# The first capped experts' front, moved beside the first scan stage chunk by chunk

## The chip, the cores and the metric

The kernel runs on one core of one Trainium2 chip. The metric is the device time of one execution in microseconds: 5519.37 us, the median of three runs (5518.34 to 5522.48). The profile is of one further execution.

## The reference, cut to what matters

Eight layers work on 4 x 1024 tokens of 256 features; each layer's result is added to its input x after a layer norm of x. The first layer is a selective scan (Mamba block), the second a mixture of eight experts with a capacity. Only these two are touched by the change:

```
x = x + mamba_block(layernorm(x), ...)      # scan over the tokens, 512 channels x 16 states
x = x + L0_ffn(layernorm(x), W_router, b_router, experts_inter, experts_out)
def L0_ffn(x):
    logits = x_flat @ W_router.T + b_router ; weights = softmax(logits)
    top_vals, top_idx = top_k(weights, 2)   ; mask = (topk_flat > 0)
    # of each expert the first `capacity` = 640 tokens, in the order of the tokens
    inputs = x_flat[used_tokens] * mask
    out = relu(inputs @ experts_inter[e]) @ experts_out[e]
    combined = zeros.at[used_tokens].add(out * weight)
```

The same experts come a second time behind the third layer (RWKV). A token's row in its expert's block depends on how many earlier tokens chose that expert, so the routing of a part of the tokens needs the counts of the parts before it.

## The kernel before, in words

The 4096 tokens stand as 32 tiles of 128 in the SBUF tile K.X. A chunk is four tiles, so there are eight chunks, 0 to 7. Each layer is a stage with a function of its own that writes one program for each engine: V is DVE, S is ACT, G is POOL, T is PE and Q is the SP queue. An engine carries its instructions out in the order written, and waits on semaphores. At the end of a stage SP waits for all semaphores of the stage and then lets the engines go on (meet_all, barrier).

The scan stage (mamba_stage, with the class Scan): a chunk has 32 units, one for each pair of channel halves and state. In a unit POOL makes the product of dt*u and B for both halves (L435, 128x1024), ACT the two decays (L402) into PSUM, DVE the two scans (L370), then DVE weighs one half with C (L377) and POOL the other (L444); in every fourth unit DVE weighs both. PE sums the weighed halves into PSUM (L477). POOL makes its products three units ahead (AHEAD = 3), the h and B/C tiles are rings of six. The SP queue issues a 512 KB broadcast of B and C for each unit, and in the first units one of 20 transfers of zeros each fourth unit.

All other work of the scan stage is placed beside the units by ticks, two for a unit (0 to 63 in a chunk). Scan.program takes the generators early, front, late and back of the chunks; each yields the tick at which it wants to go on, and `beside(tick)` runs what is due. beside is called twice in a unit on each engine. What has not come to its turn at tick 63 is issued by `beside(whole)` at the chunk's end. back(c), which is the output product of chunk c and its addition to x, is put beside the units of chunk c + 1. The work of one chunk's front (norm, input product, convolution, silu, dt) shares the two PSUM banks called front.

The experts' front is the class CappedFront. For a chunk it has these numbered steps: 0 statistics of the rows on DVE (L221, L225); 1 their factors on POOL (L233 to L244); 2 the normed rows on ACT (L1209); 3 transposes on PE (L1249) and copies on ACT (L1216); 4 the router's product on PE (L1257) and the addition of the bias on DVE (L1146). For a part of several chunks follow: 5 and 6 the softmax and the choice of two experts on DVE (L1157 to L1173, with an exponential on ACT, L1223), 6 the counting product on PE (L1267), 7 the rows' places on DVE (L1180 to L1196), and then on POOL two indirect DMAs for each tile that scatter its rows to DRAM (L1237). The helper `then` makes each DVE instruction of the routing wait for the one before it. Before the change the first experts' front stands in moe0_stage: two parts of four chunks, all behind the scan stage's barrier. finish_front runs up to four chunks in lanes, which start two rounds apart. The SP queue issues the weights of two experts at the stage's start, waits for all scatters, and then loads the first experts' rows; PE transposes these (L1436) and the experts begin. In the RWKV stage, which precedes the second experts, the front of all chunks but the last already stands beside the stage's work (`behind`), in parts of 2, 2, 2, 1 and 1 chunks.

Of the kernel before, what the change touches and what calls it, by code (L numbers as in the profile page):

```python
# [493 lines left out]
def mamba_stage(K, W):  # L494
# [3 lines left out]
    ND, PASSES = DI // P, DI // P // 2  # L498
    M = Memory(K)
# [23 lines left out]
    abs_made, soft_exp, log_made, dt_made, dtu_made, out_made, out_added = K.events(7)  # L523
    by_rows = lambda n: W["L0_attn_a_" + n].rearrange("(k p) e -> p k e", p=P)

    def sync():
# [8 lines left out]
        K.sync_constants()  # L535
        zeros = K.sync_zero_rows()
# [3 lines left out]
    def vector():  # L540
# [53 lines left out]
    def scalar():  # L594
# [71 lines left out]
        sc.scalar(dt, A, dt_made, early=early, front=front, late=late)  # L666

    def gpsimd():
# [37 lines left out]

        G.wait_ge(*vec_here.now())
        sc.gpsimd(dtu, dtu_made, early=early, front=front, late=late)

    def tensor():  # L710
        free = [turned.at(-1)] * 2

        def both_free():
            T.wait_ge(*free[0])
            T.wait_ge(*free[1])

# [43 lines left out]
        def back(c):  # L760
# [9 lines left out]
            free[:] = [out_added.at(c)] * 2  # L770

# [8 lines left out]
    K.barrier()  # L780
# [294 lines left out]
class CappedFront:  # L1075
# [6 lines left out]
    def __init__(self, K, M, W, parts):  # L1082
# [22 lines left out]
        self.centred, self.raised, self.masked, self.ranked, self.routed = K.events(5)  # L1105
# [25 lines left out]
    def vector(self, c, bank):  # L1131
        K, V, E = self.K, self.K.V, self.E
        e, o = V.e, TPC * (c - self.first[self.part_of[c]])
# [5 lines left out]
        yield 0  # L1139
        for _ in self.ln.vector_stats(c, K.X[:, chunk_tiles(c), :], 0):  # L1140
            pass
        yield 4
        i = self.part_of[c]
        V.wait_ge(*self.here.now())
        V.wait_ge(*self.logit_made.at(c))
        e.tensor_tensor(self.p[i % 2][:, o:o + TPC, :], bank(2)[:, 0:TPC * E].rearrange("p (t e) -> p t e", e=E),  # L1146
                        mid(self.rb[:], TPC), ALU.add).then_inc(*self.logit_read.up())
        if self.part(c) is None:
            return
        yield 5  # L1150
        _, n, tiles = self.part(c)
        p, a, b = (t[:, 0:n, :] for t in (self.p[i % 2], self.a, self.b))
        oh = [t[:, 0:n, :] for t in self.oh]
# [2256 lines left out]
```

## Time and profile before

| | before |
|---|---|
| median of 3 runs | 5519.37 us |
| profiled execution, device time | 5518.86 us |
| its span, first to last instruction | 5517.1 us |
| busy share: PE, DVE, ACT, POOL | 72%, 51%, 41%, 45% |
| mean granted TensorE clock | 0.841 |

A busy share is the time in which the engine had an instruction at work, over the span. The span is cut by stages: the first scan stage ends at 1020 us, the first experts' matmuls begin at 1186 us. A row of the timeline names the start, the duration, the engine, the line of the kernel, the output and inputs by tile, and how many instructions it merges; in square brackets how long the engine stood idle before it and who released it.

### The profile page before, as it was taken

How to read it: one execution, taken by the hardware profiler on the slowest of the kernel's cores; microseconds unless marked ns; L12 is line 12 of the kernel's file. 1: busy time of each engine (PE TensorE's matmuls, PEld its weight loads, DVE VectorE, ACT ScalarE, POOL GpSimd, SP SyncE). 2: the span in 40 equal slices, each digit the busy share in tenths (PEclk: the TensorE clock that was granted, in tenths of full speed). 3: DMA queues.
4: the chain of work that ended last, by engine and by line, in shares of the span. 5: the costliest groups of instructions: out<-in, count | busy, mean ns of one | idle time of the engine just before them, and what ended most of it. 6: DMA issues, size and time to landing. Idle time of an engine off the chain costs nothing.

```text
span 5517.1 us, 48791 instructions
## 1 busy us (share of the span) xinstructions
PE 3998.5 (72%) x14606; PEld 2251.6 (41%) x14608; DVE 2812.4 (51%) x5507; ACT 2234.7 (41%) x4029; POOL 2459.2 (45%) x2096
## 2 busy tenths in 40 slices
PE   6888888559757777986777199937936777778872
PEld 2333333337524455762333056634712222233552
DVE  6989999411156652117889122253244545455422
ACT  5566665211166652114555033321424444544141
POOL 5889999520133432017888400065051423222404
PEclk8999999669878888998888599958957778788896
DMA  6765555312200102224554211131442322221144
GB/s 177 199 181 143 148 141 150 96 51 95 73 16 16 29 22 71 80 68 130 136 135 139 90 60 45 43 114 75 135 108 49 58 36 43 36 36 35 66 125 133
DMA packets 356221, 494.06 MB, mean 90 GB/s; under 512 B 39481, under 2 KB 212574, under 8 KB 355886
## 3 DMA queue, kind: packets, MB, share of 16 engines
q1 hardware_dynamic: 313700, 402.60, 27.1%
q0 software_dynamic: 30720, 77.66, 4.8%
q10 hardware_dynamic: 11520, 10.49, 0.5%
q8 instruction: 123, 2.02, 0.2%
q14 instruction: 158, 1.29, 0.1%
HBM read 375.38 MB, written 121.50 MB: 90 GB/s over the span
## 4 chain that ended last, share of the span: by engine, by line
PE 31%; POOL 9%; DVE 7%; issue 6%; ACT 5%; DMA 5%; SPq 1%; POOLq 0%; DVEq 0%; ACTq 0%
PE s_gate_up L2021 7%; PE s_result_sum L2037 3%; POOL sorted_rows L943 3%; PE s_hidden_sum L1451 3%; PE s_result_sum L1462 3%; PE s_out_sum L3239 2%; PE s_scores_T L3226 2%; POOL s_gathered L963 2%; PE s_scores L3190 2%; POOL s_h L435 1%; DVE s_decay L370 1%; ACT s_weights_T L3045 1%; DMA s_rows<-sorted_rows 1%; PE s_transposed L2011 1%; DMA parts_of_max<-s_max_parts 1%
## 5 line engine op out<-in xcount | busy, mean ns | idle before, releaser
L435 POOL TENSOR_TENSOR s_h<-s_dtu,s_bc 128x1024 f32<-128x1024 f32 x384 | 901.9, 2360 | 89.7 <-PE s_y_sum L477 57.0
L477 PE MATMUL s_y_sum<-s_h,identity 128*128 128x512 f32 x1536 | 786.4, 650 | 188.0 <-POOL s_h L444 169.2
L402 ACT ACTIVATE s_decay<-s_dt,s_A 128x512 f32<-128x512 f32 x768 | 498.5, 682 | 346.5 <-DVE s_h L377 339.8
L477 PEld LDWEIGHTS s_y_sum<-s_h,identity 128*128 128x128 f32 x1536 | 298.0, 205 | 635.4 <-issue 309.0
L3045 ACT ACTIVATE s_weights_T<-s_scores_T 128x1024 f32<-128x1024 f32 (+3 forms) x384 | 300.0, 812 | 401.5 <-PE s_scores_T L3226 400.3
L2021 PE MATMUL s_gate_up<-s_w_gate_up,s_rowsT 128*128 x1184 | 422.7, 489 | 16.7 <-issue 16.5
L963 POOL DMA_INDIRECT s_gathered<-sorted_results,pick_row x192 | 199.8, 1041 | 412.1 <-SPq L113 342.2
L3109 POOL TENSOR_SCALAR_AFFINE_SELECT s_weights_T<-s_weights_T 128x256 f32<-128x256 f32 x256 | 104.0, 409 | 623.8 <-ACT s_weights_T L3045 621.6
L2080 DVE TENSOR_TENSOR s_mid<-s_act,s_gate_up 128x128 f32<-128x128 f32 (+1 forms) x228 | 92.8, 407 | 523.8 <-ACT s_act L2053 523.8
L444 POOL TENSOR_TENSOR s_h<-s_h,s_bc 128x512 f32<-128x512 f32 x256 | 325.6, 1273 | 29.4 <-DVE s_h L370 20.1
L370 DVE TENSOR_TENSOR_SCAN s_decay<-s_decay,s_carry,s_h 128x512 f32<-128x512 f32 x256 | 322.4, 1275 | 25.7 <-ACT s_decay L402 10.3
L377 DVE TENSOR_TENSOR s_h<-s_decay,s_bc 128x512 f32<-128x512 f32 x512 | 331.2, 667 | 0.0
L370 DVE TENSOR_TENSOR_SCAN s_decay<-s_decay,s_h 128x512 f32<-128x512 f32 x256 | 307.6, 1217 | 41.7 <-ACT s_decay L402 21.5
L1451 PE MATMUL s_hidden_sum<-s_rowsT,s_w_inter 128*128 128x320 f32 x1024 | 282.2, 437 | 0.9 <-ACT s_rowsT L1407 0.9
L1462 PE MATMUL s_result_sum<-s_w_exp_out,s_hidden 128*128 128x256 f32 x1280 | 279.1, 379 | 1.1 <-issue 1.1
L3190 PE MATMUL s_scores<-s_keys,s_queries 96*128 96x512 bf16 (+3 forms) x550 | 194.2, 392 | 101.3 <-DVE s_maxima L2890 26.8
L2021 PEld LDWEIGHTS s_gate_up<-s_w_gate_up,s_rowsT 128*128 128x128 f32 x1184 | 209.8, 192 | 139.9 <-issue 130.3
L2887 DVE CUSTOM_DVE_ANT_0 s_scores<-s_scores,s_mask_add 128x256 f32<-128x256 f32 (+2 forms) x380 | 189.2, 509 | 133.3 <-PE s_scores L3190 123.6
L3226 PE MATMUL s_scores_T<-s_queries,s_keys 99*128 99x512 bf16 (+3 forms) x768 | 216.2, 371 | 55.7 <-DMA s_queries<-parts_of_max 36.8
L1462 PEld LDWEIGHTS s_result_sum<-s_w_exp_out,s_hidden 128*128 128x128 f32 x1280 | 241.9, 190 | 34.3 <-issue 2.1
L1416 ACT ACTIVATE s_hidden<-s_hidden_sum 128x320 f32<-128x320 f32 x128 | 55.9, 437 | 467.5 <-PE s_hidden_sum L1451 467.5
L2890 DVE TENSOR_REDUCE s_maxima<-s_scores 128x1 f32<-128x512 f32 x170 | 117.3, 690 | 229.2 <-PE s_scores L3190 227.6
(488 smaller groups left out, 7827.8 us busy)
## 6 DMA issues: line engine op xcount, KB each, us to landing
s_bc<-s_bc_rows SPq DMA_DIRECT2D x384, 512.0 KB, 5.1
s_rows<-sorted_rows SPq DMA_DIRECT2D x228, 128.0 KB, 2.2
sorted_results<-s_result SPq DMA_DIRECT2D x228, 128.0 KB, 1.7
s_w_inter<-in_L_ffn_experts_inter SPq DMA_DIRECT2D x16, 1024.0 KB, 5.2
s_w_exp_out<-in_L_ffn_experts_out SPq DMA_DIRECT2D x16, 1024.0 KB, 8.2
s_queries<-parts_of_q SPq DMA_DIRECT2D x96, 128.0 KB, 4.6
s_keys<-parts_of_k SPq DMA_DIRECT2D x96, 128.0 KB, 7.5
sorted_rows<-zeros SPq DMA_DIRECT2D x10, 1024.0 KB
```

What stands on the lines that cost most here:

```text
L370: V.e.tensor_tensor_scan(decay if d < k else self.h[r][:, d, :], decay, self.h[r][:, d, :], self.carry[:, i, d:d + 1] if c % CPB else 0.0, ...
L377: V.e.tensor_tensor(self.h[r][:, d, :], self.decay[:, (2 * g + d) % 4, :], self.bc[r][:, 1, :], ALU.mult).then_inc(*(self.weighed_v if d = ...
L402: S.e.activation(self.decay[:, (2 * g + d) % 4, :], dt[q // self.passes % 2][:, at, :], ACT.Exp, scale=A[:, at, g % ns:g % ns + 1]).then_i ...
L435: G.e.tensor_tensor(self.h[r][:], dtu[q // self.passes % 2][:, at:at + 2, :], mid(self.bc[r][:, 0, :], 2), ALU.mult).then_inc(*self.fed.up())
L444: G.e.tensor_tensor(h, h, self.bc[g % self.RING][:, 1, :], ALU.mult).then_inc(*self.weighed_g.up())
L477: made = T.e.matmul(self.y[:, d, :], ident[:], self.h[r][:, d, :], start=False, stop=g % ns == ns - 1)
L963: G.e.indirect_dma_start(self.got[s][i][:], None, K.sorted_out, bass.IndirectOffsetOnAxis(ap=K.pick_row[i][:, t:t + 1], axis=0), bounds_ch ...
L1451: made = T.e.matmul(hb[half][:, 0:HALF], w_in[r][:, k, i * P:(i + 1) * P], xsT[r][:, k, half * HALF:(half + 1) * HALF], start=k == 0, stop ...
L1462: made = T.e.matmul(ob[n % 2][:, 0:D], hT[:, i, t * P:(t + 1) * P], w_out[r][:, i, :], start=i == 0, stop=i == KI - 1)
L2021: made = T.e.matmul(self.gb[j % 2][:, at:at + n], self.xT[j % 2][:, k, :], self.gu_flat[:, bass.ds(expert[j] * (DT * 2 * F) + (k * 2 * F + ...
L3045: S.e.activation(PT[n % 2][:, 2 * pair:2 * pair + 2, o:CH], st[pair][:, :, o:CH], ACT.Exp, scale=HD ** -0.5).then_inc(*weighed.up())
L3226: made = T.e.matmul(st[pair][:, i, o:CH], KS[u % 2][:, h, kt * P:(kt + 1) * P], QS[u % 2][:, h, qh * CH + o:(qh + 1) * CH], start=True, st ...
```

## The change

mamba_stage now makes the CappedFront for parts of 3, 3, 1 and 1 chunks and loads the router's weights. In back(c), that is beside the units of chunk c + 1, every engine carries out steps 0 to 4 of the front for chunk c, for c from 0 to 6, at ticks of a table. Where chunk c - 1 ends a part (c = 3 and c = 6), steps 5 to 7 for that part stand beside the same units: the routing and scatters of chunks 0 to 2 beside chunk 4, those of chunks 3 to 5 beside chunk 7. The routing's DVE instructions, which were one piece, each yield once. DVE's last step has half a tick between two of them. The scatters of one tile (two DMAs) stand at one tick, every second tick from 56. The front's products use the two front banks of the scan stage, and hT holds its transposed rows. POOL waits for the zero transfers before its first scatter.

The stage ends with meet_all, so its semaphores stay in use. Behind it stand the routing and scatters of chunk 6 and the whole front of chunk 7; finish_front now runs two lanes, one round apart. The routing copies both counts out of PSUM before it goes on (rank_read), one DVE instruction more for each part. Its core:

```diff
+    M0 = Memory(K)
+    moe = CappedFront(K, M0, W, (3, 3, 1, 1))
...
+    moe.xT = lambda c: hT
+    moe_bank = lambda k: bank[:, (0, 1, 0, 1)[k], :]
+    TICKS = {0: (15, 1), 1: (20, 0), 2: (22, 1), 3: (57.5, 1), 4: (61, 0), 5: (16, 1), 6: (18, 1), 7: (45, 0.5)}
+    TICKS_G, TICKS_T, TICKS_S, TICKS_V = ({**TICKS, **t} for t in ({7: (56, 2)}, {6: (44, 0)}, {3: (59, 1)}, {4: (63, 0)}))
+    def routed(c, engine, ticks, look):
+        sides = [Side(at_ticks(moe.of(engine)[0](c, look), ticks))]
+        if c and moe.part(c - 1) is not None:
+            sides.append(Side(at_ticks(moe.of(engine)[1](c - 1, look), ticks)))
+        while any(s.due is not None for s in sides):
+            tick = min(s.due for s in sides if s.due is not None)
+            yield tick
+            for s in sides:
+                s.until(tick)
...
@@ vector, back(c)
+            if c == 0:
+                V.wait_ge(*K.consts_here.at(2))
+                moe.vector_constants()
+            if c + 1 < NC:
+                yield 14
+                V.wait_ge(*out_added.at(c))
+                yield from routed(c, "V", TICKS_V, moe_bank)
@@ scalar, front(c)
+                S.wait_ge(*moe.logit_made.at(c - 3))
@@ gpsimd, a new back(c)
+            if c + 1 < NC:
+                if c == 3:
+                    yield 0
+                    G.wait_ge(*K.zeroed.at(2 * SLOT_TILES // 8))
+                yield from routed(c, "G", TICKS_G, moe_bank)
@@ tensor
+        def take(k, until):
+            f = (0, 1, 0, 1)[k]
+            T.wait_ge(*free[f])
+            free[f] = until
+            return bank[:, f, :]
...
-    K.barrier()
+    K.meet_all()
+    K.owed_front = moe, M0, [(NC - 2, True), (NC - 1, False)]
@@ CappedFront, vector_route (each instruction now behind a yield of its own)
-        then(e.tensor_copy(tot[:], totals.rearrange("p t e -> p e t")))
+        e.tensor_copy(tot[:], totals.rearrange("p t e -> p e t"))
+        e.tensor_copy(a, within).then_inc(*self.rank_read.up())
+        V.wait_ge(*self.rank_read.at(i))
@@ CappedFront, gpsimd_route
+        for t in range(tiles.start, tiles.stop):
+            yield 7
+            G.wait_ge(*self.routed.at(i))
+            r = t // TPC % self.ring
+            for j in range(2):
+                G.e.indirect_dma_start(...)
+def at_ticks(work, ticks):
+    done = {}
+    for step in work:
+        begin, pace = ticks[step]
+        yield begin + pace * done.get(step, 0)
+        done[step] = done.get(step, 0) + 1
-def moe0_stage(K, W): ...
-        rounds(lambda i: front_steps(front, chunks[i], engine, turns, work), len(chunks), 2, 4)
+        rounds(lambda i: front_steps(front, chunks[i][0], engine, turns, chunks[i][1]), len(chunks), 1, 2)
```

## Rows read from the trace of the kernel before

**Rows 1.** Windows: start:end, length, busy us and count by engine, clock, DMA share, GB/s.
```profile
181.60:307.10 125.50, 101.46 (x224) 42.65 (x224) 115.26 (x133) 68.71 (x95) 111.13 (x66) 0.91 0.73 201
...
551.70:668.20 116.50, 97.96 (x225) 41.40 (x224) 110.75 (x130) 77.91 (x150) 111.79 (x72) 0.94 0.57 144
668.20:788.60 120.40, 100.73 (x227) 41.96 (x226) 114.87 (x134) 69.01 (x96) 111.66 (x66) 0.93 0.54 141
...
903.40:1006.00 102.60, 77.28 (x172) 32.17 (x171) 102.60 (x107) 46.05 (x68) 102.60 (x57) 0.93 0.56 148
```

**Rows 2.** Groups of DVE in chunk 7: busy us, mean ns, idle us before.
```profile
L370 DVE TENSOR_TENSOR_SCAN s_decay<-s_decay,s_carry,s_h 128x512 f32<-128x512 f32 x40 | 50.2, 1272 | 0.0
```

**Rows 3.** Timeline of the gap behind the first scan: start, us, engine, line.
```profile
1020.32 0.17 DVE L1123 MEMSET s_keep<- 128x128 f32 x1 [0.20 <-SPq L113]
...
1175.62 0.97 POOL L1237 DMA_INDIRECT sorted_rows<-s_routed_xn,pick_row  x1 [0.30 <-issue]
...
1182.43 2.99 PE L1436 MATMUL s_transposed<-identity,s_rows 128*128 128x128 f32 x10 [52.51 <-DMA s_rows<-sorted_rows]
```

**Rows 4.** Timeline of the second experts' front, one chunk alone.
```profile
2118.08 1.41 DVE L221 BATCH_NORM_STATS2 s_rn_stats_routed<-residual 128x6 f32<-128x256 f32 x4 [0.38 <-SPq L113]
...
2120.06 0.23 POOL L233 TENSOR_SCALAR s_rn_minus_routed<-s_rn_meanvar_routed 128x4 f32<-128x4 f32 x1 [8.60 <-issue]
...
2130.75 0.19 DVE L1157 TENSOR_REDUCE s_route_red<-s_probs 128x4 f32<-128x32 f32 x1
...
2139.86 1.09 POOL L1237 DMA_INDIRECT sorted_rows<-s_routed_xn,pick_row  x1 [17.88 <-DVE pick_row L1196]
...
2148.92 0.97 POOL L1237 DMA_INDIRECT sorted_rows<-s_routed_xn,pick_row  x1 [0.31 <-issue]
...
2155.65 2.99 PE L1436 MATMUL s_transposed<-identity,s_rows 128*128 128x128 f32 x10 [20.36 <-DMA s_rows<-sorted_rows]
```

**Rows 5.** Timeline of the last units of the first scan.
```profile
997.95 1.27 DVE L370 TENSOR_TENSOR_SCAN s_decay<-s_decay,s_carry,s_h 128x512 f32<-128x512 f32 x1
...
998.11 4.71 POOL L435 TENSOR_TENSOR s_h<-s_dtu,s_bc 128x1024 f32<-128x1024 f32 x2
...
1000.90 1.27 DVE L370 TENSOR_TENSOR_SCAN s_decay<-s_decay,s_carry,s_h 128x512 f32<-128x512 f32 x1
1001.01 1.30 ACT L402 ACTIVATE s_decay<-s_dt,s_A 128x512 f32<-128x512 f32 x2 [1.65 <-DVE s_h L377]
...
1002.73 3.75 POOL L444 TENSOR_TENSOR s_h<-s_h,s_bc 128x512 f32<-128x512 f32 x3
```

**Rows 6.** Timeline of another stage's routing, DVE beside POOL.
```profile
3731.66 1.26 POOL L2564 TENSOR_TENSOR s_shared_mid<-s_shared_act,s_shared_copies 128x512 f32<-128x512 f32 x1 [2.00 <-ACT s_shared_copies L2542]
3731.68 1.79 DVE L879 SCALAR_TENSOR_TENSOR s_route_a<-s_onehot,s_route_a 128x512 f32<-128x512 f32 x1
```

**Rows 7.** Timeline of the attention stage, DVE beside POOL.
```profile
4116.21 2.35 POOL L3081 TENSOR_TENSOR s_crossed<-s_crossed,s_sin 128x1024 f32<-128x1024 f32 x1
...
4116.48 4.85 DVE L980 SCALAR_TENSOR_TENSOR residual<-s_gathered,pick_weight,residual 128x256 f32<-128x256 f32 x2
...
4118.64 2.40 POOL L3084 TENSOR_TENSOR s_straight<-s_straight,s_crossed 128x1024 f32<-128x1024 f32 x1
```

**Rows 8.** Timeline of POOL in the second scan stage, two gathers.
```profile
2706.66 1.04 POOL L1005 DMA_INDIRECT s_pair<-sorted_results,pick_row  x1 [0.16 <-POOL s_h L435]
2708.01 1.00 POOL L1005 DMA_INDIRECT s_pair<-sorted_results,pick_row  x1 [0.30 <-issue]
2709.03 2.37 POOL L435 TENSOR_TENSOR s_h<-s_dtu,s_bc 128x1024 f32<-128x1024 f32 x1
```

**Rows 9.** Timeline of the gap: ACT's copy and DVE's logit addition.
```profile
1028.98 0.60 ACT L1216 ACTIVATE s_routed_xT<-s_transposed 128x512 f32<-128x512 f32 x1 [0.26 <-PE s_transposed L1249]
...
1033.38 0.19 DVE L1146 TENSOR_TENSOR s_probs<-s_hidden_sum,s_b_router 128x32 f32<-128x32 f32 x1 [6.84 <-PE s_hidden_sum L1257]
```

**Rows 10.** Groups up to 1300 us: a routing instruction of 128 elements.
```profile
L1193 DVE TENSOR_TENSOR s_route_b<-s_onehot,s_route_a 128x128 f32<-128x128 f32 x4 | 1.2, 292 | 0.1
```

More of the change, by code:

```diff
@@ L664, in late, with back @@
             log_term(2 * c + 1)
-        sc.scalar(dt, A, dt_made, early=early, front=front, late=late)
+        def back(c):
+            if c + 1 < NC:
+                yield from routed(c, "S", TICKS_S, moe_bank)
+        sc.scalar(dt, A, dt_made, early=early, front=front, late=late, back=back)
     def gpsimd():
@@ L770, in back @@
             free[:] = [out_added.at(c)] * 2
+            if c + 1 < NC:
+                if c == 0:
+                    T.wait_ge(*K.consts_here.at(2))
+                yield from routed(c, "T", TICKS_T, take)
         T.wait_ge(*a_exp.at(1))
@@ L1155, in vector, with then @@
         weight = [w[:, tiles] for w in K.pick_weight]
+        def then(inst):
+            inst.then_inc(*self.step.up())
+            V.wait_ge(*self.step.now())
+        yield 5
         V.wait_ge(*self.logit_read.at(c))
         then(e.tensor_reduce(red, p, AX.X, ALU.max))
+        yield 5
         e.tensor_tensor(p, p, last(red, E), ALU.subtract).then_inc(*self.centred.up())
@@ L1281, in next, with front_steps @@
         return self.n[engine] % len(self.banks)
-def front_steps(front, c, engine, turns, work):
+def front_steps(front, c, engine, turns, routing_only=False):
     mine = {}
@@ L1297, in take @@
         return turns.banks[f][:]
-    side = Side(work(c, take if engine == "T" else look) if engine != "G" else work(c))
-    for i in range(front.STEPS):
+    chunk, route = front.of(engine)
+    bank = take if engine == "T" else look
+    sides = [] if routing_only else [Side(chunk(c, bank))]
+    if front.part(c) is not None:
+        sides.append(Side(route(c, bank)))
+    for i in range(5 if routing_only else 0, front.STEPS):
         for k in {3: (0, 1), 4: (2,), 6: (3,) if front.part(c) else ()}.get(i, ()):
             mine[k] = turns.next(engine)
-        side.until(i)
+        for side in sides:
+            side.until(i)
         yield
+def at_ticks(work, ticks):
[4 more added lines that the diff above has]
+        done[step] = done.get(step, 0) + 1
 def rounds(chunk, n, skew, lanes):
@@ L1388, in vector @@
     def vector():
-        finish_front("V", front.vector)
+        finish_front("V")
         for e in range(E):
@@ L1400, in scalar @@
     def scalar():
[L1401 removed]
+        finish_front("S")
         def rows_turned_copy(e):
@@ L1546, in look, with behind @@
         return of.banks[of.next(engine)]
-    def behind(c, engine, work):
+    def behind(c, engine):
         if c + 1 < NC:
-            yield from front_steps(moe, c, engine, turns, work)
+            yield from front_steps(moe, c, engine, turns)
     def sync():
@@ L1718, in chunk @@
             V.wait_ge(*added.at(4 * c + 3))
-            yield from behind(c, "V", moe.vector)
+            yield from behind(c, "V")
         rounds(chunk, NC, SKEW, 2)
@@ L1835, in chunk @@
                 yield
-            yield from behind(c, "S", moe.scalar)
+            yield from behind(c, "S")
         rounds(chunk, NC, SKEW, 2)
@@ L1876, in chunk @@
                 yield
-            yield from behind(c, "G", moe.gpsimd)
+            yield from behind(c, "G")
         rounds(chunk, NC, SKEW, 2)
@@ L1947, in chunk @@
                 yield
-            yield from behind(c, "T", moe.tensor)
+            yield from behind(c, "T")
         rounds(chunk, NC, SKEW, 2)
```

113 lines of the change are left out of this document (63 added, 50 removed).

## The prediction, made before the changed kernel ran

> **What bounds the kernel now.** I read the page first, then the windows by scan chunk, then the groups and the timeline of the first scan stage and of the gap behind it. The windows [rows 1] have one line for each of the eight 512-token chunks of the first scan (chunks 1, 4, 5 and 7 are shown, by the line's start) and one for the stretch between that stage's end and the first expert's work. In chunks 4 and 5 DVE is busy 110.75 of 116.5 and 114.87 of 120.4 us and POOL 111.79 and 111.66: two engines are full at once, and they feed each other (POOL's product feeds DVE's scan, POOL weighs what DVE scanned). Chunk 1 leaves both 10 to 14 us. In chunk 7 DVE never waits [rows 1, 2]. The gap is the opposite: from 1020.32 to 1182.43, 162.1 us, no engine is full; it is one chain of norm, logits, routing and scatter that ends on POOL's indirect DMAs, last issued at 1175.62 [rows 3]. The change takes work out of the slack stretch and puts it into the full one. So the question is the exchange rate.
>
> **The gap.** What stays behind the scan is the routing and scatter of chunk 6 and the whole front of chunk 7. The second experts' stage of this same kernel shows a front of one chunk alone: first DVE instruction 2118.08, first POOL factor 2120.06, routing begun 2130.75, first scatter 2139.86 (8.3 us of DVE for four tiles and 0.8 for POOL to start), the eighth 2148.92 (1.28 to 1.29 us each), first expert transposes 2155.65 [rows 4]. That is 37.6 us. In the changed kernel POOL issues chunk 6's eight scatters before chunk 7's factors, since the earlier lane runs first in each round. Those scatters wait for 8.3 us of routing, 1.8 of chunk 7's statistics in its midst and 0.8 to start: about 11 us, then 8 x 1.28 = 10.2. The factors begin at 21.2 instead of 2.0 us, 19.2 later, so the gap becomes 56.8 us. Saved: 105.3. The expert weights are issued at the stage's start as before and have these 57 us to land.
>
> **The stage's end.** The new end is meet_all over the same events, among them the scatter semaphores. The second route's scatters (12 tiles, 24 DMAs) begin at tick 56 of chunk 7, one pair for two ticks. The chunk has ticks 0 to 63, so four pairs fit and the other 16 DMAs are issued in one burst when the chunk's units are over. In the other scan stage a pair of gathers stands so between POOL's products and takes it 2.4 us from the first to the next product [rows 8], with 0.15 ahead of it. Four pairs are 8 x 1.28 = 10.2 us, the burst is 16 x 1.28 = 20.4 [rows 4]. POOL's last product of the scan ended at 1006.48 [rows 5]. Put behind it, 10.2 + 20.4 us and 1.3 to land give 1038.4, against 1020.3: 18 later. If DVE has been slowed more than POOL, POOL stands up to 6 us earlier relative to it, and the end is 12 later. I take 14, nearer to the second. Net gain behind the scan: 105.3 - 14 = 91.3.
>
> **What every chunk from 1 to 7 gets.** DVE: four statistics (1.41 us together [rows 4]), four aggregates and the logit add, an estimated 2.1 us. POOL: four small factor instructions, 1.9. ACT six, PE 24. A new wait: DVE's logit add stands at tick 63. ACT's second copy stands at tick 60, behind the two decays that wait for DVE's unit 30. Two decays take 1.3 us (at 1001.01) [rows 5], and from that copy's start to DVE's add the gap shows 4.4 (1028.98 to 1033.38) [rows 9]: 5.7 us after unit 30, while unit 31, whose weighing falls to DVE twice, takes about 3.5 (a unit's 2.95 and 0.6). DVE stands 2.3 us, and its next scan, ACT's next decays and POOL's next weighing are queued behind it. Together 4.4 a chunk. It passes whole in 3, 5 and 6, and half in 1 and 2: 3 x 4.4 + 2 x 2 = 17.2. Bounds: 8 (absorbed) and 30 (POOL and PE work added in full as well).
>
> **The two routes beside the scan** (chunks 4 and 7). A route is 37 DVE instructions; at 96 elements I take 0.27 us each, from 0.292 at 128 [rows 10] and 8.3 us for the whole at 32: 10 us. But 26 of them read two SBUF tiles, and the scan's own DVE instructions never do: they read one operand from PSUM. Beside a large POOL tensor_tensor such an instruction waits until POOL's has ended. L879 starts at 3731.68, POOL's 1.26 us product at 3731.66; L879 takes 1.79 and ends 0.55 behind it [rows 6]. Two in a row at 4116.48 take 4.85, over two POOL products of 2.35 and 2.40 [rows 7]: each waits for one. In the scan POOL has a 2.37 us product and a 1.27 us one in nearly every unit [rows 5].
>
> So a DVE unit of 2.95 us (997.95 to 1000.90 [rows 5]; 3.1 in the mean of four, since one of four has the second weighing) becomes the following. Let s be the end of its second scan, which releases POOL. Ticks 16 to 32, one instruction per half unit: the first waits for POOL's weighing, s + 1.6; scan, s + 2.75; the second waits for the product, s + 4.05; scan, s + 5.2. With only one of the two affected it is 4.2 to 5. Mean 4.85 against 3.1 in chunk 7, eight units: 14 us. Ticks 45 to 54, two instructions per half unit: s + 1.6, s + 4.1, scan, two free ones, scan, s + 7.0; 3.6 more than 3.1 in 4.5 units, less 1.5 for reductions: 15. With 0.7 for tick 17 the route costs 30 us in chunk 7. In chunk 4 the twelve convolution terms stand between the instructions of ticks 23 to 32 and ACT's waits cover some: 10 + 15 = 25. Bounds: 10 each (no wait), and 10 + 26 x 1.85 = 58 each (a POOL product is always in the way; POOL would have to be busy without end while DVE, which releases it, stands).
>
> **Chunk 4 in addition.** The rank matmuls stand at PE's tick 44 behind ACT's silus of tick 43, and DVE's tick 45 waits: 3 us (0 to 5). And 24 scatters: four pairs and the burst, 10.2 + 20.4 = 30.6 us of POOL. POOL has products for three units ahead. It trails DVE's need by some 5 us of lead, gains about 4 while DVE is slow and 2.3 in the logit wait. What is left, 19 us, is a stall of DVE at the start of chunk 5 (12 to 28). Chunk 4: 4.4 + 25 + 3 + 19 = 51.4. Chunk 7: 4.4 + 30 = 34.4; its burst is counted above.
>
> **A trap that I weigh and leave at nothing.** The scatters' descriptors: in the other scan stage the second gather of a pair started 1.35 us after the first, beside DVE's scans [rows 8], the pace of the gap. The Trainium skill, "SBUF — State Buffer", the warning on DVE blocking software DMAs, says that GpSimd can't write descriptors while DVE runs a 2-port mode. By it alone each of 48 scatters could stand behind a DVE instruction; the trace's pair shows none of it beside scans that read PSUM, and the scatters start at tick 56, behind the route's last instruction.
>
> The same page, "Who interferes with whom", also lists copy, cast and tensor_scalar as contending. Five more instructions of each route would then wait, and by an estimate of 1.2 us each the sum would be 12 us higher, 5542. No row here shows a large POOL instruction beside one of these.
>
> **The sum.** Scan stage + (17.2 + 51.4 + 34.4) = +103.0. Behind it - 91.3. Together + 11.7 on the profiled execution's own 5518.86 us, which is 0.5 under the median of the runs: 5530.
>
> **The rivals.**
> First, faster: DVE's waits for POOL don't build up. DVE and POOL fall into step, so that the short instructions land where POOL stands. For it: the 26 are short, and a stalled DVE starves POOL. Then a route costs its own 10 us, chunk 7 is 20 less and chunk 4 15 to 18 less: 5493. If the burst at chunk 4 is also half hidden by POOL's lead, 5484. Against it: the two consecutive instructions [rows 7], each behind a whole product.
> Second, much faster: the slack of [rows 1] takes the fixed additions and most of the stall, only the routes' own time is left: scan + 50, so 5478. Against it: DVE idle 0.0 in chunk 7 [rows 2].
> Third, slower: the end of DVE's waits is not where I put it. POOL is itself held by DVE's reads (about 0.2 us each) and works on without a pause after chunk 4's burst, which then drags through chunk 5 since POOL has only 8.7 us to give there [rows 1]: burst 28 instead of 19, routes 8 more each, fixed additions 25: + 33, 5563. It decides if POOL's lead is gone at the burst.
> That the change doesn't do what it says, the scatters left behind the scan: they are on POOL's list at fixed ticks, I give it nothing.
>
> **How the numbers follow.** The forecast's case 0.45, with its own range 5512 to 5548; the first rival 0.28; the second 0.07; the third 0.20. A measurement of this kernel tells about 0.2%, 11 us, from no change. The forecast's case gives slower 0.21, same 0.19, faster 0.05; the first rival faster 0.23, same 0.05; the second faster; the third slower 0.19, same 0.01. Together faster 0.35, same 0.25, slower 0.40. The range 5484 to 5562 leaves out about one in ten at either side.
>
> **What would show it.** First expert transposes about 57 us after the stage's end instead of 162; the stage's end near 1137 instead of 1020, with 16 scatters in a row before it. In chunks 4 and 7 L1166 to L1193 take 1 to 2.5 us each instead of 0.27, more in ticks 45 to 54. DVE stands some 19 us at the start of chunk 5 for POOL's product, with 16 scatters on POOL. DVE's logit add waits about 2 us in seven chunks. It is wrong if the route's instructions keep 0.3 us beside POOL's products (then 5493), or if the scan grows by more than 130 us.

## The result, and the profile after

The changed kernel takes 5536.91 us (median of 8 runs, 5528.94 to 5550.35) against 5520.92 of the kernel before (8 runs, 5518.27 to 5528.0). The ratio is 1.0028, with a 95% interval of 1.0016 to 1.0040: some 16 us slower. The profiled execution took 5535.33 us, with a span of 5533.4.

The first view is the windows of the kernel after, one line for each of chunks 1, 4, 5, 6 and 7 of the first scan, each cut at the chunk's first scan instruction. The columns are those of [rows 1].

```profile
180.40:315.00 134.60, 110.48 (x247) 48.98 (x248) 119.81 (x147) 71.95 (x101) 115.17 (x72) 0.84 0.70 189
566.70:713.50 146.80, 112.22 (x252) 49.55 (x252) 135.61 (x175) 81.62 (x158) 114.71 (x77) 0.86 0.43 116
713.50:862.90 149.40, 105.12 (x249) 46.92 (x250) 117.11 (x142) 71.83 (x101) 135.85 (x92) 0.85 0.48 133
862.90:985.60 122.70, 103.76 (x249) 47.03 (x250) 110.96 (x130) 77.61 (x149) 112.42 (x70) 0.90 0.53 138
985.60:1121.00 135.40, 93.54 (x199) 39.24 (x200) 130.84 (x153) 47.96 (x72) 108.09 (x65) 0.84 0.44 115
```

Chunk 4 pays on DVE (135.6 us busy, 110.8 before), chunk 5 pays on POOL (135.9, 111.7 before). The same cut gives the length of each chunk in every run below:

| us | 0 | 1 | 2 | 3 | 4 | 5 | 6 | 7 | scan | from last scan to experts |
|---|---|---|---|---|---|---|---|---|---|---|
| before | 121.4 | 125.6 | 125.4 | 119.2 | 116.4 | 120.4 | 114.8 | 102.6 | 945.8 | 176.1 |
| after | 120.1 | 134.6 | 126.0 | 125.6 | 146.8 | 149.4 | 122.8 | 135.3 | 1060.6 | 83.0 |
| more | -1.3 | 9.0 | 0.6 | 6.4 | 30.4 | 29.0 | 8.0 | 32.7 | 114.8 | -93.1 |

The two stages together are 21.7 us longer. The span grew by 16.3, so the stages behind them differ by some 5 us between these two executions.

How a routing instruction stands beside POOL, first DVE, then POOL, in chunk 7. L1228 ends some 0.1 us behind POOL's product, at 1056.75 against 1056.63; L1233 meets a POOL that stands, and takes 0.24.

```profile
1056.00 0.75 DVE L1228 TENSOR_TENSOR s_onehot<-s_route_b,s_route_red 128x96 f32<-128x96 f32 x1
...
1057.98 0.24 DVE L1233 TENSOR_TENSOR s_route_b<-s_onehot 128x96 f32<-128x96 f32 x1
```

```profile
1054.28 2.35 POOL L435 TENSOR_TENSOR s_h<-s_dtu,s_bc 128x1024 f32<-128x1024 f32 x1
1059.62 1.26 POOL L444 TENSOR_TENSOR s_h<-s_h,s_bc 128x512 f32<-128x512 f32 x1 [2.99 <-DVE s_h L370]
```

The timeline of POOL and DVE at the start of chunk 5: the first burst, and DVE's wait for it. In POOL's part 13 of the 16 DMAs of the burst are left out.

```profile
722.07 2.38 POOL L435 TENSOR_TENSOR s_h<-s_dtu,s_bc 128x1024 f32<-128x1024 f32 x1
724.61 1.01 POOL L1316 DMA_INDIRECT sorted_rows<-s_routed_xn,pick_row  x1 [0.17 <-issue]
...
727.20 0.98 POOL L1316 DMA_INDIRECT sorted_rows<-s_routed_xn,pick_row  x1 [0.30 <-issue]
...
743.82 0.97 POOL L1316 DMA_INDIRECT sorted_rows<-s_routed_xn,pick_row  x1 [0.30 <-issue]
744.79 2.37 POOL L435 TENSOR_TENSOR s_h<-s_dtu,s_bc 128x1024 f32<-128x1024 f32 x1
```

```profile
713.48 0.19 DVE L1189 TENSOR_TENSOR s_probs<-s_front,s_b_router 128x32 f32<-128x32 f32 x1 [2.50 <-PE s_front L1336]
...
726.86 0.67 DVE L377 TENSOR_TENSOR s_h<-s_decay,s_bc 128x512 f32<-128x512 f32 x1
747.20 2.47 DVE L370 TENSOR_TENSOR_SCAN s_decay<-s_decay,s_carry,s_h 128x512 f32<-128x512 f32 x2 [19.68 <-POOL s_h L435]
```

Four pairs came before, with a product behind each. From 724.61 to 744.79 POOL issues 16 DMAs in a row and nothing of the scan, and DVE stands 19.7 us.

The groups of DVE in chunk 7, each shape apart: routing instructions on 96 elements. The first three wait, the last three do not.

```profile
L1224 DVE TENSOR_TENSOR s_route_b<-s_route_b,s_reversed_iota 128x96 f32<-128x96 f32 x2 | 3.2, 1594 | 0.0
L1261 DVE TENSOR_TENSOR s_route_a<-s_route_a,s_first_row 128x96 f32<-128x96 f32 x1 | 2.3, 2291 | 0.0
...
L1272 DVE CAST pick_row<-s_route_slot 128x12 int32<-128x12 f32 x2 | 2.1, 1070 | 0.0
...
L1226 DVE TENSOR_REDUCE s_route_red<-s_route_b 128x12 f32<-128x96 f32 x2 | 0.5, 227 | 0.0
...
L1263 DVE SCALAR_TENSOR_TENSOR s_route_a<-s_route_b,s_route_a 128x96 f32<-128x96 f32 x1 | 0.2, 241 | 0.0
L1217 DVE TENSOR_TENSOR s_probs<-s_probs,s_route_red 128x96 f32<-128x96 f32 x1 | 0.2, 240 | 0.0
```

All groups of routing lines (L1208 to L1272) add up to 26.0 us of DVE in chunk 7 and to 23.1 in chunk 4, with 4.3 us of standing before the count is read there. The same lines on tiles of the same size, with POOL quiet, stand in the run that puts the second route behind the scan: L1224 and L1263 take 0.26 us there, L1272 0.17.

The groups of the two lines of DVE that wait for PE, over the whole program. Of L599 (the multiplication by z at the end of a pass) the kernel before shows 10.5 us of waiting in the same group, of which 7.6 lie inside the scan; now it is 32.3, and 25.9. The six waits of the logit addition are 2.03 to 2.51 us, 2.27 in the mean.

```profile
L1189 DVE TENSOR_TENSOR s_probs<-s_front,s_b_router x7: 178/192/192, 315.1 to 1122.2; 128x32 f32<-128x32 f32 x7
...
  PE s_front L1336: 13.6, 6
```

```profile
L599 DVE TENSOR_TENSOR s_u<-s_y_sum,s_z 128x1024 f32<-128x1024 f32 x16 | 19.5, 1219 | 32.3 <-PE s_y_sum L477 32.3
```

The timeline behind the scan, the counterpart of [rows 3] and [rows 4]: the end of the burst, the new stage's first instruction, chunk 6's eight scatters (six left out), the factors of chunk 7 behind them, and the first expert transposes.

```profile
1143.71 0.97 POOL L1316 DMA_INDIRECT sorted_rows<-s_routed_xn,pick_row  x1 [0.30 <-issue]
1147.62 0.19 DVE L1208 TENSOR_REDUCE s_route_red<-s_probs 128x4 f32<-128x32 f32 x1 [9.16 <-SPq L113]
...
1158.42 0.97 POOL L1316 DMA_INDIRECT sorted_rows<-s_routed_xn,pick_row  x1 [13.74 <-DVE pick_row L1272]
...
1167.36 0.97 POOL L1316 DMA_INDIRECT sorted_rows<-s_routed_xn,pick_row  x1 [0.31 <-issue]
1168.41 0.24 POOL L233 TENSOR_SCALAR s_rn_minus_routed<-s_rn_meanvar_routed 128x4 f32<-128x4 f32 x1
...
1204.06 2.25 PE L1525 MATMUL s_transposed<-identity,s_rows 128*128 128x128 f32 x8 [20.53 <-DMA s_rows<-sorted_rows]
```

From the stage's first instruction to the transposes it is 56.4 us.

### The profile page after: what moved, and what is told of

Same layout as the page of the kernel before. It is cut to its first block, busy times and chain, and to the rows that moved or that the text cites. A ratio compares the mean times of both kernels' runs of the same rounds, so it can differ in the third digit from the quotient of the medians.

```text
span 5533.4 us, 48942 instructions
## 1 busy us (share of the span) xinstructions
PE 4026.9 (73%) x14612; PEld 2258.7 (41%) x14612; DVE 2855.5 (52%) x5590; ACT 2235.8 (40%) x4031; POOL 2455.3 (44%) x2096
## 4 chain that ended last, share of the span: by engine, by line
PE 31%; POOL 9%; issue 6%; DVE 6%; ACT 5%; DMA 5%; SPq 1%; POOLq 0%; DVEq 0%; ACTq 0%
PE s_gate_up L2110 7%; PE s_result_sum L2126 3%; POOL sorted_rows L992 3%; PE s_hidden_sum L1540 3%; PE s_result_sum L1551 3%; PE s_out_sum L3328 2%; PE s_scores_T L3315 2%; POOL s_gathered L1012 2%; POOL s_h L435 2%; PE s_scores L3279 2%; ACT s_weights_T L3134 1%; DMA s_rows<-sorted_rows 1%; DMA parts_of_max<-s_max_parts 1%; DVE s_decay L370 1%; PE s_transposed L2100 1%
## 5 line engine op out<-in xcount | busy, mean ns | idle before, releaser
L477 PE MATMUL s_y_sum<-s_h,identity 128*128 128x512 f32 x1536 | 803.3, 661 | 199.1 <-POOL s_h L444 152.2
L435 POOL TENSOR_TENSOR s_h<-s_dtu,s_bc 128x1024 f32<-128x1024 f32 x384 | 901.7, 2358 | 97.9 <-PE s_y_sum L477 74.2
L402 ACT ACTIVATE s_decay<-s_dt,s_A 128x512 f32<-128x512 f32 x768 | 498.6, 682 | 411.9 <-DVE s_h L377 405.3
L2110 PE MATMUL s_gate_up<-s_w_gate_up,s_rowsT 128*128 x1184 | 422.2, 489 | 17.6 <-issue 17.1
```

Of the source, the lines that this page charges most:

```text
L402: S.e.activation(self.decay[:, (2 * g + d) % 4, :], dt[q // self.passes % 2][:, at, :], ACT.Exp, scale=A[:, at, g % ns:g % ns + 1]).then_i ...
L435: G.e.tensor_tensor(self.h[r][:], dtu[q // self.passes % 2][:, at:at + 2, :], mid(self.bc[r][:, 0, :], 2), ALU.mult).then_inc(*self.fed.up())
L477: made = T.e.matmul(self.y[:, d, :], ident[:], self.h[r][:, d, :], start=False, stop=g % ns == ns - 1)
L2110: made = T.e.matmul(self.gb[j % 2][:, at:at + n], self.xT[j % 2][:, k, :], self.gu_flat[:, bass.ds(expert[j] * (DT * 2 * F) + (k * 2 * F + ...
```

## The experiments

The ten ran in three groups, each on a chip of its own, and on each the kernel before is slower than in the first measurement: 5616.41 us in the first group (the four edits by themselves), 5608.75 in the second (the probe, the control and the two combinations), 5605.69 in the third (the pieces). The changed kernel was run again in the second group alone. There its two stages take the same time as on the first chip: 1144.5 us from the first scan to the first expert transposes against 1143.6. The extra time lies behind them. Comparisons below are ratios to the kernel before on the same chip, and lengths from the traces; a comparison of ratios from different groups is also one of different chips.

### The factors first

```diff
     def gpsimd():
-        finish_front("G")
+        for c, routing_only in chunks:
+            if not routing_only:
+                Side(front.gpsimd(c, None)).until(9)
...
+        for c, _ in chunks:
+            if front.part(c) is not None:
+                Side(front.gpsimd_route(c, None)).until(9)
```

> The changed kernel, with one thing altered behind the scan: POOL issues the norm factors of chunk 7 before the eight scatters of chunk 6. My theory (chunk 7's front waits 19 us on POOL's list for scatters that nothing in it needs): the stretch from chunk 7's addition to x to the first expert transposes shrinks from 65.6 us to about 47, the end of the program moves by the same 19 us, 5537 to 5518. Rival (the stretch ends on the 16 scatters themselves, 20.5 us of POOL, which only change places with the factors): less than 5 us. Second rival (the copies, transposes and the router's product then wait for something of chunk 6): about 10 us.

5614.8 us, ratio 0.9999 (0.9988 to 1.0010). POOL's timeline behind the scan (scatters left out):

```profile
1154.30 0.24 POOL L233 TENSOR_SCALAR s_rn_minus_routed<-s_rn_meanvar_routed 128x4 f32<-128x4 f32 x1 [10.28 <-issue]
...
1158.90 1.08 POOL L1316 DMA_INDIRECT sorted_rows<-s_routed_xn,pick_row  x1 [2.65 <-DVE pick_row L1272]
...
1174.11 0.97 POOL L1316 DMA_INDIRECT sorted_rows<-s_routed_xn,pick_row  x1 [5.18 <-DVE pick_row L1272]
```

The factors stand at 1154.30 instead of 1168.41, and from the last scan to the expert transposes it is 69.3 us instead of 83.0: 13.7 less, where 19 was expected. The order on POOL is the cause, but it doesn't act whole. Chunk 7's statistics stand behind half of chunk 6's routing on DVE, so the factors come 6.2 us after the stage's first instruction (1148.11) and not 2 as in [rows 4]; POOL also stands 5.2 us for chunk 7's routing before the last eight scatters. From that first instruction it is 41.6 us instead of 56.4, 14.8 less; the other 1.1 us were lost before it, where DVE's last addition to x began 8.9 us after PE's product for it had ended (see the last section). For the same reason the stretch that the expectation names, from that addition, is no measure: it is 43.1 us.

### The burst spread out

```diff
+        SLOTS = {4: (56, 58, 60, 62), 5: (8, 22, 36, 50), 6: (8, 22, 36, 50), 7: (56, 58, 60, 62, 64, 64, 64, 64, 64, 64, 64, 64)}
...
+                    owed.append(work)
...
+                for tick in sorted(SLOTS.get(c + 1, ()) + (20.5,)):
```

> The changed kernel, with the eight tiles of scatters that came in one burst at the end of chunk 4 spread out: four tiles over chunk 5 and four over chunk 6, a pair for each 14 ticks. Theory (the burst of 16 takes POOL's lead of three units away and DVE stands 19.7 us): that stall goes, chunks 5 and 6 take up the pairs in POOL's idle time (13 and 10 us in them), each chunk pays 2 to 4 us for the rest; the scan is 14 to 20 us shorter, 5537 to about 5520. Rival (POOL is full all along, and the scatters cost their own 20.5 us wherever they stand): no change within 4 us, chunks 5 and 6 each 10 us over the kernel before instead of 29 and 8.

5614.27 us, ratio 0.9994 (0.9982 to 1.0006). The windows of chunks 5 and 6 of this run:

```profile
715.30:845.80 130.50, 102.16 (x250) 45.78 (x249) 117.32 (x143) 72.12 (x104) 127.11 (x82) 0.95 0.53 143
845.80:968.00 122.20, 100.92 (x249) 45.98 (x248) 111.07 (x131) 77.42 (x148) 119.62 (x77) 0.93 0.52 148
```

Chunk 5 fell from 149.4 to 130.5, chunk 6 did not grow (122.8 to 122.2) though POOL took up eight more DMAs in it. The scan is 19.5 us shorter. The same 24 scatters cost 19 us less when POOL has a product between the pairs: the burst was a stall, not work.

### The second route behind the scan

```diff
-        if c and moe.part(c - 1) is not None:
+        if c == 3:
...
-    K.owed_front = moe, M0, [(NC - 2, True), (NC - 1, False)]
+    K.owed_front, K.owed_starts = (moe, M0, [(5, True), (6, True), (7, False)]), (0, 3, 1)
```

> The changed kernel with the second route (chunks 3 to 5: 37 DVE instructions and 24 scatters) taken from beside chunk 7 and put behind the scan, ahead of chunk 6's; the factors of chunk 7 first on POOL. Theory (a route beside the scan costs 25 us through waits for POOL, behind it 10 us that lie in a chain): chunk 7 falls from 135.3 to about 110 us, the stage's end no longer waits for a burst (12 us less), and the stretch behind grows to some 70 us from the stage's end. Against the changed kernel about 22 us less, 5515; against the run with the factors first alone, 3 us less. Rival (the route beside the scan is cheap and the growth of chunk 7 is POOL's and PE's added work): chunk 7 keeps 125 or more and the time is 5525 or more.

5619.58 us, ratio 1.0013 (1.0000 to 1.0025). Chunk 7 of this run:

```profile
986.00:1093.40 107.40, 82.15 (x198) 36.16 (x197) 102.75 (x115) 47.67 (x71) 100.59 (x58) 0.93 0.52 135
```

Chunk 7 is 107.4 us instead of 135.3, 27.9 less: that is what a route and its four pairs of scatters cost there. It is 4.8 us over the kernel before, which is this chunk's share of the fixed additions. The rival, that chunk 7 grew by other work, has fallen. Behind the scan it is 93.4 us instead of 83.0. From the stage's first instruction it is 77.6, where some 70 were expected; POOL stands 8 us there before its last eight scatters (the last section). The two stages are 20.4 us shorter than in the changed kernel; by the control's 1.0029 (below) that would make 0.9993, and more than half of the gain is missing in the measured ratio. This kernel also has the factors first. Against the run with that alone, on the same chip, 3 us less were expected; the two stages are 5.7 us shorter, but the ratio is 0.14% higher, with an uncertainty of 0.17%. The time of the whole kernel is thus a miss, and its cause stays open.

### ACT's copies and PE's product earlier

```diff
-    ... {6: (44, 0)}, {3: (59, 1)}, {4: (63, 0)}))
+    ... {6: (44, 0), 4: (59, 0)}, {3: (57, 0)}, {4: (63, 0)}))
```

> The changed kernel with ACT's two copies of the transposed rows at tick 57 instead of 59 and 60, and PE's router product at tick 59 instead of 61. Theory (PE stands with the scan's sums queued behind the router's product, which waits for ACT's second copy; DVE's logit addition, 2.3 us in each of six chunks, and its multiplication by z, 22 us more than in the kernel before, wait for that): both waits go nearly whole, 25 to 34 us, 5537 to about 5508. Rival (DVE and POOL are full, and what DVE no longer waits for there it waits for elsewhere): 0 to 10 us. Second rival (ACT's copies ahead of the decays hold DVE's next scan): slower by up to 10 us.

5622.27 us, ratio 1.0011 (1.0002 to 1.0020). The logit addition no longer waits at all (13.6 us before), L599 waits 17.0 us inside the scan (25.9). That is 22.5 us of waiting gone, but the scan is only 8.1 shorter: 3.1 in chunk 1, 3.9 in chunk 3, 5.7 in chunk 6, and chunks 4 and 7 are 0.9 and 2.5 longer. My theory named two waits that the edit does shorten and took them for the price; part of what DVE saved it stood elsewhere (its addition to x waits 6.8 us instead of 3.0, the costliest group of its scans 28.3 instead of 24.9 for POOL). The rival holds. The edit took 8.9 of the 18.3 us that were added before L599, so half of them has another source.

### Which instructions wait for POOL

```diff
...
+            for n in range(32 if c + 1 in PROBE else 0):
+                yield 16 + n
+                V.wait_ge(*step_p.now())
+                PROBE[c + 1]().then_inc(*step_p.up())
```

> The kernel before with 32 small instructions added on DVE in each of five chunks of the first scan, one for each half unit from tick 16 to 47, all on 128x96 floats in SBUF: a product of two tiles in chunks 2 and 6, a reduction in chunk 3, a copy in chunk 4, a multiplication by a constant in chunk 5 (the outputs are not part of the computation). Theory (an instruction that reads two SBUF tiles waits for POOL's running product, one that reads one tile does not): the products take 0.8 us or more in the mean against 0.25 for the reduction, and chunk 6 grows by 15 us or more, chunk 3 by 8 at most. Rival (copies and multiplications by a constant wait as well, as one cast of 1.07 us and one multiplication of 1.44 us in the changed kernel suggest): these two kinds also take 0.5 us or more in the mean. Second rival (the long ones of the routes came from the chain of dependences, not from POOL): all kinds take 0.3 us or less.

One execution, 5713.92 us. DVE's groups of the added lines, by kind (L542 chunk 2, L543 chunk 3, L544 chunk 4, L545 chunk 5, L546 chunk 6):

```profile
L544 DVE COPY s_probe<-s_probe 128x96 f32<-128x96 f32 x32 | 37.0, 1156 | 0.0
L546 DVE TENSOR_TENSOR s_probe<-s_probe 128x96 f32<-128x96 f32 x32 | 33.0, 1030 | 0.0
L545 DVE TENSOR_SCALAR s_probe<-s_probe 128x96 f32<-128x96 f32 x32 | 29.6, 924 | 0.0
L542 DVE TENSOR_TENSOR s_probe<-s_probe 128x96 f32<-128x96 f32 x32 | 24.5, 764 | 0.0
L543 DVE TENSOR_REDUCE s_probe<-s_probe 128x12 f32<-128x96 f32 x32 | 7.6, 236 | 0.0
```

Against the kernel before, chunk 2 grew by 20.2 us, chunk 3 (reductions) by 4.1, chunk 4 (copies) by 30.8, chunk 5 (multiplications by a constant) by 23.9 and chunk 6 by 29.1. So it is the kind that decides, and not the number of tiles read: copies and multiplications by a constant wait as products of two tiles do, reductions don't wait. Each kind but one has a chunk of its own, and the products differ between their two chunks (0.76 and 1.03 us), so the sizes can't be ranked; but of the 32 reductions none took over 0.25 us, and most of them ended while a product of POOL still ran. My theory was half right, the first rival holds, the second has fallen.

### The control

> The changed kernel itself, unaltered, as the measure for the others of this group on the same chip: 1.0028 of the kernel before by the first measurement, with 0.12% to either side.

5625.75 us, ratio 1.0029 (1.0016 to 1.0041), as on the first chip. So the run with the factors first (0.9999) is 0.30% under the changed kernel, the spread scatters 0.35%, the second route behind 0.16%, the earlier copies 0.18%. Each of these differences is between two chips and uncertain by 0.15 to 0.18%: the first two are clear of noise, the last two are not, or barely.

### The edits together, with one route and with two

The first takes the four edits above at once. The second keeps the second route beside chunk 7 and issues eight of its tiles behind the stage's end: three ahead of the factors, five after.

> Four edits at once on the changed kernel: the first route's scatters spread over chunks 4, 5 and 6; the second route and its scatters behind the scan; the factors of chunk 7 first on POOL; ACT's copies and PE's router product two ticks earlier. Theory (the terms are separate): scan 1061 less 19 (burst), 28 (second route), 8 (copies) = 1006 us, behind it some 90 us to the first expert transposes; 48 us less than the changed kernel and 26 less than the kernel before, ratio 0.995. Rival (the terms share the same stall, so that the second saves little once the first is gone): 1.000. Second rival (later stages give the time back, as between the first experts and the second ones in the runs so far, where 14 to 20 us less shrank to 5): 0.998.

5578.73 us, ratio 0.9949 (0.9936 to 0.9962), as expected: the terms are separate, and no later stage gives them back. Scan 998.2, 8 us under the theory's 1006, behind it 93.1. The two stages are 30.7 us shorter than in the kernel before, the time is 30.0 less.

> As the combined kernel, but with the second route beside chunk 7 as in the changed kernel, four of its twelve tiles scattered there and the other eight behind the stage's end: three before the factors of chunk 7 on POOL, five after them. Theory: scan 1034 us, behind it no burst holds the stage's end and POOL works without a pause, 63 us from the last scan to the first expert transposes; total 5 us above to 5 us below the combined kernel. Rival (the burst was hidden behind the output product, and what is left over only follows later): behind the scan 69 us as in the run with the factors first, 6 to 10 us above the combined kernel.

5581.4 us, ratio 0.9952 (0.9939 to 0.9966). Scan 1035.7, behind it 64.1: the theory's 1034 and 63. It is 2.7 us over the version with one route, which the noise does not separate.

### The routes in pieces

```diff
-    ... {4: (63, 0)}))
+    ... {4: (63, 0), 5: (16, 0), 6: (18, 0), 7: (48, 0)}))
```

The table is DVE's: for each step the first tick and the ticks between two instructions.

> The combined kernel (one route beside the scan), with the route's DVE instructions in two pieces instead of one for each half unit: 20 in a row at tick 18, 17 in a row at tick 48. Theory (each instruction that reads SBUF waits at most for the POOL product that runs, and POOL has products only for some three units before it needs DVE again, so in a long piece only the first few wait): the route takes 9 us of its own and waits for about three POOL instructions in each piece, some 16 us in all against 25; with the wait for the counting product (4 us) gone as well, chunk 4 falls from 147.0 to about 135 us and the time by 10 us. Rival (POOL's lead is lost in the standing time and DVE waits for it afterwards): chunk 4 at 143 or more. Second rival (every instruction of a piece waits for a product, as two in a row do in the attention stage): chunk 4 above 150.

5578.67 us, ratio 0.9945 (0.9928 to 0.9961). Chunk 4 went from 147.0 to 141.8, not to 135, and the time of the whole did not fall by the 10 us expected: 0.9945 against 0.9949 can't be told apart.

> The kernel with both routes beside the scan, with both in two pieces each in the same way. Theory: chunk 4 as in the run with one piece, chunk 7 from 140.0 to about 126; 25 us less than the same kernel with the instructions spread, ratio about 0.991, and so ahead of the version with one route. Rival (lost lead): chunk 7 at 136 or more, ratio 0.994 or more. Second rival (each waits): above 0.998.

5565.55 us, ratio 0.9923 (0.9907 to 0.9938): the lowest ratio of all, 40 us under the kernel before on its chip. Against the same kernel with the instructions spread that is 0.29%, some 16 us, where 25 were expected; the two stages are 15.0 us shorter. Its timeline of DVE and of POOL in chunk 4, in the first piece (twelve instructions left out):

```profile
593.34 2.87 DVE L1223 TENSOR_TENSOR s_probs<-s_probs,s_route_red 128x96 f32<-128x96 f32 x1
...
600.25 1.15 DVE L1230 TENSOR_TENSOR s_probs<-s_probs,s_route_red 128x96 f32<-128x96 f32 x1
...
601.72 0.26 DVE L1235 TENSOR_TENSOR s_route_b<-s_probs,pick_weight 128x96 f32<-128x96 f32 x1
602.01 0.26 DVE L1237 TENSOR_TENSOR s_route_b<-s_route_b,s_reversed_iota 128x96 f32<-128x96 f32 x1
...
604.92 0.26 DVE L1248 SCALAR_TENSOR_TENSOR s_mask<-s_probs,s_route_b 128x96 bf16<-128x96 f32 x1
```

```profile
591.44 4.65 POOL L435 TENSOR_TENSOR s_h<-s_dtu,s_bc 128x1024 f32<-128x1024 f32 x2
...
598.94 2.34 POOL L435 TENSOR_TENSOR s_h<-s_dtu,s_bc 128x1024 f32<-128x1024 f32 x1
606.69 1.27 POOL L444 TENSOR_TENSOR s_h<-s_h,s_bc 128x512 f32<-128x512 f32 x1 [5.40 <-ACT s_carry L414]
```

L1230 waits until POOL's product of 598.94 has ended at 601.28. Then POOL's weighing, which comes behind a scan of DVE by way of ACT's s_carry, stands 5.4 us, and nothing of the piece waits any more. L1223 stands alone between scans and takes 2.87, until the second of two products that followed each other without a gap has ended (596.09). The routing lines take 15.9 us in chunk 4 (25.8 spread out) and 17.7 in chunk 7 (32.3). Chunk 7 gets it whole, 140.0 to 124.0: the theory's 126. In chunk 4 the routing lines take 9.9 us less and the counting wait of 4.2 is gone as well, but the chunk is only 5.3 shorter. POOL is busy 116 us in it, spread out or in pieces. What the trace shows is that DVE waits 7.5 us for ACT there, 6.3 of them for the decays (L402), and none in the spread version; the kernel before has such waits in chunk 4 as well (4.6 and 1.2). So the spread instructions had covered waits that the pieces lay open again, as the forecast had put it for chunk 4. The rival, that DVE waits for POOL afterwards, has fallen: there is no such wait in the chunk.

## Why the prediction was right, point by point

The time: 5530 was predicted, with slower at 0.40 as the likeliest of the three; it is 5536.91. Scan + 103.0 predicted, + 114.8 measured; behind it - 91.3 predicted, - 93.1 measured. For the two stages together that is + 11.7 against + 21.7. (The forecast's sum is 5530.6, which it wrote as 5530.) That the time came out within 7 us is in part luck: the fixed additions were 16 us too low, the chunks of the routes took back 4, chunk 0 1, the stretch behind the scan 2, and 5 came from the stages behind, for which nothing was forecast.

- **The gap.** 56.8 us from the stage's start predicted, 56.4 measured, with the factors behind chunk 6's scatters as the reason. The factors came 20.8 us after the stage's start (21.2 predicted), the transposes 35.7 after them (35.6 in [rows 4]). The run with the factors first showed the reason, at 13.7 us instead of 19.2: the template of [rows 4] has the statistics at once, here half a routing stands ahead of them on DVE.
- **The stage's end.** It moved from 1020.32 to about 1147.6, 127.3 us; 114.8 of it is the scan, so 12.5 is the burst, against 14 (12 to 18). The sign to look for was an end near 1137; the scan's growth made it 10 later.
- **The burst in chunk 5.** 19 us predicted, 19.68 measured, 18.9 recovered by spreading it.
- **The routes.** 25 and 30 us predicted. The routing lines are busy 23.1 and 26.0 us; chunk 7 grew by 32.7 (34.4 predicted), and a route with four pairs of scatters was worth 27.9 there. Chunk 4 grew by 30.4 (32.4 predicted without the burst). The mechanism holds, the counting was wrong in three ways. A route has 21 instructions that read two SBUF tiles, not 26; one comes to 26 with the three operations with a constant and the two casts, which the estimate of 5542 then adds once more. Those five can wait too: the probe shows 1.16 us for copies and 0.92 for multiplications by a constant in the mean, and the cast in the profile after takes 1.07. The Trainium skill, "SBUF — State Buffer", section "Who interferes with whom", lists copy, cast and tensor_scalar as instructions that can contend; the trace agrees. With them the sum was 5542, and the time lies between the two sums, but not for that reason: the routes cost no more than forecast. For instructions wait less often than I put it: of the 21 in chunk 7 seven took 0.30 us or less, since no large product of POOL was at work beside them, as the first rival had it in part.
- **The fixed additions.** This is the term that was mis-sized. Chunks 1, 2, 3 and 6 grew by 24.0 us together, 12.8 predicted (2, 2, 4.4, 4.4). Chunk 5 grew by 29.0, which leaves 9.3 without its 19.7 of burst (4.4 predicted); with the burst spread out it grew by 10.1. The five chunks thus have 33.3 us instead of 17.2, and the upper bound, 30, did not hold. The logit wait was 2.27 us in the mean of six chunks, 2.3 predicted, but in chunk 7 there was none. What I had left out is DVE's multiplication by z, L599: DVE waits 18.3 us more for PE's sums inside the scan. The run with the earlier copies showed that about half of this comes from the router's product ahead of those sums, and that not all of it is a price: 22.5 us of both waits gone gave 8.
- **Chunk 1** alone has 9.0 us instead of 2. Two things of it can be read. The forecast had put the front's constants at nothing: they are made there, and two short instructions on 8 elements (L1176, L1177) take 3.0 us there (rows below). And DVE waits 7.6 us before L599 there, 3.0 in the kernel before. That wait goes with the clock: the granted clock of chunk 1 was 0.84 after and 0.91 before, and over the runs chunk 1 grew by 5.9 to 9.0 us where its clock was 0.84 to 0.86, and by 2.2 to 7.5 where it was 0.90 to 0.93. No run tells which is the cause of which.

```profile
L1176 DVE TENSOR_SCALAR s_reversed_iota<-iota 128x8 f32<-128x8 f32 x1 | 1.7, 1694 | 0.1
...
L1177 DVE TENSOR_SCALAR s_first_row<-iota 128x8 f32<-128x8 f32 x1 | 1.3, 1308 | 0.0
```

- **The counting wait.** 4.3 us, 3 predicted.
- **The trap left at nothing.** The scatter pairs beside the scans start 1.3 us apart (713.69 and 715.01 on POOL), the pace of the gap (the first pair 1.5). DVE's scans did not hold them up.

The third rival (5563: burst 28, routes 8 more each, fixed additions 25) fell on the burst, 19.7, and on the routes; on the fixed additions it was nearer than the forecast's own case. The first rival's place, where short instructions land while POOL stands, exists: it is what the pieces use.

What stays open: 5 us between the two profiled executions behind these stages, half of the added wait before L599, and the spread of chunk 1 between runs in which nothing or two ticks were altered there.

## What to carry to other kernels

Where two full engines feed each other and a short instruction of one waits for a long one of the other, a chain of short instructions did better in two pieces than one by one: spread out, each can meet a long instruction anew, in one piece the other engine runs out of work and the rest is free. It gave 16 us of chunk 7 and 5 of chunk 4, where the spread instructions had covered waits for a third engine. Software DMAs are the opposite: in one piece they take the lead away from whoever waits for that engine's next product, in pairs between products eight of them cost chunk 6 nothing. And a wait that is seen on the fullest engine is not its price: take it away and see what the stage gives back.

## What the runs showed of the hardware that was not expected

- On DVE beside POOL's products, a copy of 128x96 floats in SBUF took 1.16 us in the mean and a multiplication by a constant 0.92, as much as products of two tiles (0.76 and 1.03); a reduction kept 0.24. In the routes of the changed kernel the two copies that read PSUM (L1241, L1242) kept 0.25 to 0.26 while L435 ran on POOL.
- The waiting instructions end just behind POOL's: 0.11 to 0.12 us for nearly all products of two tiles in chunks 4 and 7 of the changed kernel, 0.03 for the casts, 0.06 to 0.07 for the probe's copies.
- A waiting instruction is held by more than one POOL instruction if these follow each other without a gap: L1223 took 6.49 us in chunk 7 of the run with two routes spread, and 5.07 in that with the pieces. In the probe the first copy took 5.90, over four products of POOL.
- In seven of the ten traces of kernels with the change, DVE took up its work after the PE product that it needed had ended, 1.9 to 17.6 us late, while POOL issued scatters one after another. Below is the combined kernel with one route: PE's product ended at 1107.4 and DVE's addition began at 1122.74. Nothing in the trace names the cause ("remote"), and it was not tested. There, in the run with the second route behind the scan (14.1 us late) and in that with one piece (17.6), POOL then stood 8 to 9 us before its last eight scatters. It isn't fixed by the program: the control's last addition to x was 4.6 us late, the same kernel's on the first chip was on time.

```profile
1103.79 3.58 PE L1349 MATMUL s_transposed<-s_w_router,s_routed_xT 128*128 128x8 f32 x16 [0.69 <-ACT s_routed_xT L1307]
```

```profile
1095.12 0.17 DVE L1285 CAST pick_row<-s_route_slot 128x4 int32<-128x4 f32 x1
1122.74 0.19 DVE L1202 TENSOR_TENSOR s_probs<-s_transposed,s_b_router 128x32 f32<-128x32 f32 x1 [27.45 <-remote]
```
